# The opening of an attention stage: half-size weight loads, plain matmuls ahead of the first projection, and one score pair moved

## What is computed

```
xs = x * condT / sqrt(128)               (per sequence)
u  = (xs @ w0) / sqrt(sum((w0*s)^2)+eps) (demodulated)
q, k, v = u @ W_qkv                      (16 heads of 64)
p  = softmax(mask(q k^T / 8));  o = p @ v
x  = x + o @ W_out
f, i, h = gates of x;  scan over the 128 tokens
```

## Time and profile before

| | |
|---|---|
| median of 3 runs | 1012.3 us |
| the profiled execution: its own time | 1013.4 us |
| its span | 1012.1 us |
| PE busy | 969.6 us, 96% of the span |
| DVE busy | 869.5 us, 86% |
| ACT busy | 838.4 us, 83% |
| POOL busy | 488.1 us, 48% |
| granted TensorE clock, mean | 0.997 |

### The profile page before, as it was taken

How to read it: one execution, slowest core, us unless ns; L and a number is a source line. 1 busy time by engine, 2 the same in 40 slices (tenths; PEclk the granted TensorE clock), 3 DMA queues, 4 the chain that set the end, 5 groups by cost and what they waited for, 6 DMA issues and landing times.

```text
span 1012.1 us, 25907 instructions
## 1 busy us (share of the span) xinstructions
PE 969.6 (96%) x8939; PEld 789.5 (78%) x8939; DVE 869.5 (86%) x3687; ACT 838.4 (83%) x2232; POOL 488.1 (48%) x572
## 2 busy tenths in 40 slices
PE   7999999999999999899989999999999999999897
PEld 6899999998989899633268988888777777776566
DVE  6777989898989899599998999888989888896985
ACT  6999889898989889677797878776888888886786
POOL 2444656564646464416810112102888888893041
PEclk9999999999999999999999999999999999999999
DMA  9000000000000000000000000000000000000002
GB/s 381 31 2 2 2 2 2 2 2 1 3 2 2 2 2 2 1 1 1 1 1 1 1 1 1 1 11 12 22 23 23 23 23 22 24 3 2 1 1 84
DMA packets 8722, 18.30 MB, mean 18 GB/s; under 512 B 1296, under 2 KB 5648, under 8 KB 8208
## 3 DMA queue, kind: packets, MB, share of 16 engines
q1 hardware_dynamic: 8592, 16.65, 4.9%
HBM read 10.36 MB, written 2.10 MB: 12 GB/s over the span
## 4 chain that ended last, share of the span: by engine, by line
PE 69%; DVE 17%; ACT 6%; POOL 4%; issue 4%; DMA 0%; ACTq 0%; DVEq 0%; POOLq 0%
PE PB L258 7%; PE PB L259 6%; PE PB L260 6%; PE PB L1874 5%; PE PB L399 5%; PE PB L416 4%; PE PB L360 4%; PE PB L1259 3%; PE PB L1261 3%; PE PB L1260 3%; PE PB L1846 3%; PE PB L1891 3%; DVE AR_s L328 2%; DVE W L370 2%; PE PB L1904 1%
## 5 line engine op out<-in xcount | busy, mean ns | idle before, releaser
L258 PE MATMUL PB<-RR_s 128*128 128x256 f32 (+3 forms) x568 | 190.3, 335 | 4.8 <-POOL RR_s L479 1.9
L259 PE MATMUL PB<-RR_s 128*128 128x256 f32 (+3 forms) x568 | 176.8, 311 | 0.0
L260 PE MATMUL PB<-RR_s 128*128 128x256 f32 (+3 forms) x568 | 176.7, 311 | 0.0
L379 ACT ACTIVATE W<-W,small 128x128 f32<-128x128 f32 x384 | 149.0, 391 | 15.8 <-DVE small L370 15.8
L391 POOL TENSOR_TENSOR W<-W,small 128x512 f32<-128x512 f32 x96 | 100.1, 1046 | 105.9 <-DVE small L385 105.9
L1862 POOL TENSOR_TENSOR AR_s<-AR_s,small 128x512 f32<-128x512 f32 x128 | 129.4, 1041 | 15.1 <-DVE small L1855 14.9
L258 PEld LDWEIGHTS PB<-RR_s 128*128 128x128 f32 x568 | 108.4, 191 | 22.4 <-issue 8.8
L1233 ACT ACTIVATE AR_s<-PB,W 128x512 f32<-128x512 f32 (+2 forms) x160 | 100.5, 629 | 28.6 <-PE PB L260 22.7
L1247 DVE TENSOR_TENSOR RR_s<-AR_s,RR_s 128x512 fp32r<-128x512 f32 (+2 forms) x160 | 100.4, 637 | 17.0 <-ACT RR_s L1238 13.8
L1855 DVE CUSTOM_DVE_ANT_0 AR_s<-PB,W 128x128 f32<-128x128 f32 x512 | 111.2, 286 | 2.0 <-issue 0.2
L259 PEld LDWEIGHTS PB<-RR_s 128*128 128x128 f32 x568 | 108.6, 191 | 4.5 <-issue 0.5
(11 more groups left out here) (392 smaller groups left out, 2600.1 us busy)
## 6 DMA issues: line engine op xcount, KB each, us to landing
W<-in_w SPq DMA_DIRECT2D x1, 5809.5 KB, 24.5
W<-in_w SPq DMA_DIRECT2D x2, 1024.0 KB, 6.8
out<-XT SPq DMA_DIRECT2D x8, 256.0 KB, 2.3
XF<-in_xT SPq DMA_DIRECT2D x3, 512.0 KB, 9.9
W<-AR_s SPq DMA_DIRECT2D x16, 64.0 KB, 2.1
AR_s<-AR_s SPq DMA_DIRECT2D x16, 64.0 KB, 2.1
QS<-AR_s SPq DMA_DIRECT2D x12, 64.0 KB, 2.1
KR<-AR_s SPq DMA_DIRECT2D x12, 64.0 KB, 2.1
```

The lines of the kernel that those rows point to most:

```text
L258: nc.tensor.matmul(out, lh, rh, start=True, stop=False)
L259: nc.tensor.matmul(out, ll, rh, start=False, stop=False)
L260: return nc.tensor.matmul(out, lh, rl, start=False, stop=True)
L379: e = nc.scalar.activation(SS[r][:, hl], SS[r][:, hl], ACTF.Exp, bias=mx[r][:, h:h + 1], scale=-1.0, accum_out=rc[r][:, h:h + 1])
```

## The change

Five edits in the opening, and one that acts in the whole stage:

- wq and wk are stored as two halves (`wqk0`: the first 512 columns of each, `wqk1`: the last), loaded by two transfers of 512 KB with a semaphore each. The loads of x behind them are cut differently (1024 and 2048 columns instead of three times 1024).
- The factor -1/8 moves out of the weights' high and low parts into the maximum (`dve_max`), whose scale was 1.0; the mask's sign turns. `dve_weights` becomes a plain subtraction.
- Three of six low parts of weights go from DVE to POOL (`pool_weights`, entries 2 to 4), and the last one (entry 5) moves behind `dve_rc(1)` of period 0.
- The ten transposes become two groups of six plain 128x128 matmuls of ones, one ahead of the demodulation and one behind u.
- The fourth `pe_k` and its copy `dve_qk(3)` go behind the scores of units 0 and 1 and their maxima. ACT makes the first weights' high part ahead of `act_uh(0)`, and loads the exponential's table after the second.
- In every period `act_pt(4z-1)` now stands ahead of `act_xh`, where there is one.

```
-        nc.sync.dma_start(W1[:, 0:o_v], w_d[:, 0:o_v]).then_inc(s_w[0], 16)
+        nc.sync.dma_start(W1[:, 0:o_k], w_d[:, 0:o_k]).then_inc(s_w[0], 16)
+        nc.sync.dma_start(W1[:, o_k:o_v], w_d[:, o_k:o_v]).then_inc(s_w[4], 16)
...
+        def pool_weights(i):
+            name, at, landed, h, hi, lo = WEIGHTS[i]
+            pool.wait_ge(s_wh, i + 1)
+            nc.gpsimd.tensor_tensor(cs(lo, h), cs(w(name), at), cs(hi, h), ALU.subtract).then_inc(s_const, 1)
...
-                nc.vector.tensor_tensor_reduce(SS[r][:, hl], score(u, h), w("mask"), 1.0, 3.0e38, ALU.add, ALU.min,
+                nc.vector.tensor_tensor_reduce(SS[r][:, hl], score(u, h), w("mask"), -0.125, 3.0e38, ALU.add, ALU.min,
...
         def pe_attend():
+            pe.wait_ge(s_const, 4)
+            for k in range(6):
+                nc.tensor.matmul(PB[4][:, 0:128], ones, ones, start=True, stop=True)
             pe.wait_ge(s_set, 3)
             nc.tensor.matmul(PB[6][:, 0:32], w2, ys2, start=True, stop=True).then_inc(s_dem, 1)
             pe_u(0)
-            for k in range(10):
-                nc.tensor.transpose(PB[4][:, 0:128], ident, ident)
+            for k in range(6):
+                nc.tensor.matmul(PB[4][:, 0:128], ones, ones, start=True, stop=True)
             pe.wait_ge(s_dem, 2)
-            for n in range(4):
+            for n in range(3):
                 pe_k(n)
             for z in range(NP - 1):
                 for u in range(4 * z, 4 * z + 4):
+                    if u == 2:
+                        pe_k(3)
                     pe_S(u)
...
             nc.scalar.activation(dT, PB[6][:, 0:32], ACTF.Sqrt, bias=c_eps8).then_inc(s_dem, 1)
+            act_weights(0)
             act_uh(0)
-            for i in range(6):
+            act_weights(1)
+            nc.scalar.activation(pads[:, 2:3], pads[:, 3:4], ACTF.Exp)
+            for i in range(2, 6):
                 act_weights(i)
-            nc.scalar.activation(pads[:, 2:3], pads[:, 3:4], ACTF.Exp)
...
+                if z:
+                    act_pt(4 * z - 1)
                 for s in split_steps(2 * z + 1):
                     act_xh(*s)
-                if z:
-                    act_pt(4 * z - 1)
...
             dve_uf(0)
+            dve_weights(0)
             dve_ul(0)
-            dve_weights(0)
             dve_weights(1)
-            for n in range(4):
-                dve_weights(2 + n)
+            for n in range(3):
                 dve_qk(n)
             for z in range(NP):
                 dve_max(4 * z)
                 if z:
                     dve_rc(4 * z - 1)
                 dve_max(4 * z + 1)
+                if z == 0:
+                    dve_qk(3)
+                    dve_rc(0)
                 dve_max(4 * z + 2)
...
                 dve_rc(4 * z + 1)
+                if z == 0:
+                    dve_weights(5)
...
             pool_xs(0)
+            for i in range(2, 5):
+                pool_weights(i)
             pool_xs(1)
```

59 lines of the change are left out of this document (34 added, 25 removed).

## The result

| | before | after | ratio, 95% interval |
|---|---|---|---|
| median, us | 1012.97 (1011.80 to 1014.03, 7 runs) | 1017.34 (1014.54 to 1018.26, 7 runs) | 1.0032 (1.0020 to 1.0044) |
| the same kernel once more | 1013.53 (32 runs) | 1016.25 (1014.81 to 1018.16, 11 runs) | 1.0025 (1.0014 to 1.0036) |
| profiled execution, us | 1013.4, span 1012.1 | 1014.81, span 1013.5 | |
| mean granted clock | 0.997 | 0.997 | |

The forecast was 1013.5 with a range to 1015.6. The change makes the kernel **slower, by 2.7 to 4.4 us** at the medians; by the ratios it is 0.25 and 0.32%, about 2.5 and 3.2 us, with both intervals above 1. And yet the profiled execution came out where the sum had put it, at 1014.81 against 1014.6. That execution is among the shortest of its kernel.

The account below looks back on a forecast made before the run. From about 38 us PE's own work was taken as the bound, so the opening only makes everything start sooner. Reordering +2.89 less opening 1.67 is +1.22: 1014.6 us profiled, 1013.5 for the median, range 1010.1 to 1015.6.

Parts of the forecast that it names:

- rival 4: Opening: the half load brings nothing, first projection at 9.4, opening worth 0.4, 1014.8 us; chance 0.12.
- The clock, 2.4 GHz from 8.2 on: PE in the opening: matmuls of ones raise the clock early, 2.4 GHz from 8.2 us; other bound 9.6.
- The new wait: Opening: units 2 and 3 wait for DVE's fourth copy behind eight maxima; 1.9 of 3.55 us won given back.
- Scores of period 1, 20.91: PE, end of the opening: these scores start at 20.91 instead of 22.59 us, 1.68 earlier.
- Rival 3: Opening: ACT's earlier first exponential counts, gain 3.55 us, 1011.6 with the reordering; chance 0.08.
- Period 5, +0.53: Reordering in period 5: act_xh later, PE's gate projection at 82.12 instead of 81.59, +0.53 us.
- Periods 9 and on, 0.22 each: Reordering in periods 9, 13 to 29: act_xh 0.22 us later, all counting on PE, six times, +1.32.
- rival 1: The reordering is absorbed by PE's small waits in the next periods, 1010.6 us; chance 0.20.
- Period 31, +1.04: Reordering in the last period: POOL's low part of x, on the chain that ended last, 1.04 us later.
- The whole reordering, +2.89: act_pt ahead of act_xh over all periods: the period terms together cost 2.89 us.
- the opening is worth 1.67: All edits of the opening together: 1.67 us gained, 1.1 if the clock rises only at 9.6.
- Rival 2: Opening: matmuls of ones count no more than transposes, PE at 1.2 GHz until about 13.4, 1015.5 us; chance 0.13.

Follow-up runs that it names:

- xh_first: The changed kernel with the reordering undone, act_xh ahead of act_pt again, new opening kept: 1011.9 us (12 runs), ratio 0.9992.
- pt_first_only: The kernel before with only the reordering, act_pt ahead of act_xh, old opening kept: 1016.06 us (8 runs), ratio 1.0029.
- after_transposes: The changed kernel with the old warm-up, ten transposes in place of the matmuls of ones: 1016.12 us (12 runs), ratio 1.0016.
- look_b2: The kernel before, unedited, one more profiled execution: 1016.59 us.
- look_b3: The kernel before, unedited, another single profiled execution: 1012.63 us.
- look_a2: The changed kernel, unedited, one more profiled execution: 1016.2 us.
- xh_fill: xh_first with 14 instead of 6 matmuls of ones in the second warm-up group: 1012.55 us (12 runs), ratio 1.0001.
- look_a4: The changed kernel, unedited, another single profiled execution: 1016.17 us.
- after_fill: The changed kernel with 14 instead of 6 matmuls of ones ahead of the first projection (the filled kernel): 1017.48 us (11 runs), ratio 1.0026.

## Why the prediction was wrong, step by step

- **First projection, 8.19.** Right: 8.47 in the profile, 8.19 to 8.81 in the five executions, up to 9.23 in xh_first, as the load comes. The half load does what it should, and rival 4 is out.
- **The clock, 2.4 GHz from 8.2 on.** It was up by then in all fourteen executions with the matmuls of ones, between 4.2 and 7.3 us, though it did not stay up in all. No run shows the other bound, a rise at 9.6.
- **First scores 10.70, first maximum 11.92.** 10.92 and 12.13, the 0.2 to 0.3 of the first projection carried on.
- **The new wait.** Right: the copy ends at 14.52 (forecast 14.30), the next copies start at 17.47 (17.26).
- **Scores of period 1, 20.91.** 21.16 in the profile, so -1.43 of the forecast -1.67, of which 1.32 is the load. Rival 3, ACT's head start, is out: ACT waits 2.46 us for the first value projection, behind its eight exponentials, as was argued against it.
- **Period 5, +0.53.** From its scores to the next it takes 13.95 instead of 13.32 us, +0.63. **Periods 9 and on, 0.22 each.** 14.38 instead of 14.16 in period 9, and 0.2 in the others; but the period behind each is 0.1 shorter (13.05 instead of 13.14), so rival 1, the absorption, was right for about half of this term. Together +1.46 (+1.41 against xh_first) of the forecast 1.85.
- **Period 31, +1.04.** The low part is 0.98 later. Where no clock falls near 423 us the rest is 0.8 longer (608.3 in pt_first_only, 607.5 in xh_first).
- **The whole reordering, +2.89.** pt_first_only gives +2.9 with an interval from 1.4 to 4.4. By the parts it is 1.3 and 0.8, so 2.1 where no clock falls; what more there is comes with the fall near 423 us, which the sum did not have.

**The step that failed** is the term "the opening is worth 1.67", with "I take 2.4 GHz from 8.2 us on" under it, as a gain kept in every execution. Both ends of it were wrong. On the side of the changed kernel the clock does come up early, and then it falls again at about 15 us in three of five executions. The fall costs 0.95 us before the scores of period 1, which then stand at 22.12 to 22.45, and 0.5 more in period 1: 1.5 us gone of 1.67. On the side of the kernel before, the trace that I read had a late rise, at 13.5; in two of three executions it is up by 8.6, with the scores of period 1 at 22.43 and 21.98. Part of the forecast gain was in the kernel already.

By the middle values of the table the opening is worth 0.3 (22.43 to 22.12), not 1.67, the middle part costs 1.8 (381.09 to 382.86), and the rest 1.3 (608.5 to 609.8). That is +2.8, against +2.7 and +4.4 measured at the medians, and inside both ratios' intervals. With all executions that share an opening, four old ones and eight new ones, the opening is worth 0.8 (22.5 to 21.7), half of the term, less what a fall costs in period 1. What stays in every execution is the earlier load; the rest of the opening gained 0.1 us at most.

This accounts for the size of the miss and not for all of the spread. The filled kernel had no fall at 15 us in three executions and has the same median, and six runs of the changed kernel are longer than any that was profiled. How much of the medians the fall makes stays open.

The Trainium skill, page "TensorE: Matmul & The Clock Gate", Part 4, was cited for transposes that do not count as activity of PE. The one trace I had agreed with it as far as it went. The runs do not bear it out: with only ten transposes behind two products of 0.6 and 1.2 us the clock was up at 7.8 (after_transposes, during the last transpose), 8.6 (look_b2) and 8.4 (look_b3), and in three other executions of such an opening at 12.6, 13.5 and 13.9. The measurement decides: the clock can come up while PE transposes, and it did so early in three of six executions. How much the two products ahead of the transposes have to do with it no run separates. With the matmuls it was up between 4.2 and 7.3 us in all fourteen profiled executions that have them. Rival 2, matmuls of ones that count for nothing, is out.

A second, smaller fault: the term for period 31 was priced by the shift alone. The same shift of 1 us moves a wait of 2.7 us on PE, and along with it the clock falls near 423 us in ten of eleven executions, where it fell in four of nine; that the shift is the reason was not tested by itself. Without a fall up to 430 us the rest was 607.4 to 607.6 us with the high parts first and 608.3 with the transposed weights first, so without a fall the shift cost 0.8 of the forecast 1.04. With a fall near 423 us, none at 411 and none at 759 it was 608.5 and 609.0 in the one order, and 609.8 to 610.1 in the other.

A third is how the number was put on the median: 1.1 us below the profiled execution because before stood so. The changed kernel's median stands 2.5 above its profiled execution. One execution of each kernel says what the chain does, not how often the clock falls.

What stays open: the fall at 15 us follows the wait of 1.57 us, but a fill of that wait alone, of the right length, was not tried. Among the eight executions of the new opening, those with the fall had the rise at 4.5 to 5.0 us and those without it at 4.2 and at 5.8 to 7.3; so when the clock rose may matter, and eight are too few to tell. And the opening without the reordering is 1.6 and 1.0 us under the kernel before at the medians of two comparisons whose intervals both contain 1 (0.9992 and 0.9990): likely a gain, not a shown one. xh_first has the lowest median of this study, with 1011.9 against 1016.25 for the changed one beside it.

## What to carry to other kernels

A step that is put behind another one on its engine is paid for on the engines that wait for it, even if its own engine loses nothing: half a microsecond of ACT's order cost 2.1 us on PE and POOL by the traces, and 2.9 by the timed runs. Cut every trace at two or three fixed instructions and compare the parts of several executions before you trust a gain of 1 to 2 us; one trace of each kernel would have called this change +1.4. And a gain that creates idle time on PE in front of dense work has to carry the risk that the clock falls there: it did in four executions of fourteen with such a wait, though it was not shown that the wait is the cause.

## What the runs showed of the hardware

- The granted clock of one and the same program changes at other times in each execution: up at 13.5, 8.6 or 8.4 us in the kernel before; at 4.2 to 6.6 in the changed one, with or without a fall at 15. Without that fall the time from the scores of period 1 to the last scores hardly knows of it: 0.13 us of spread over nine executions.
- The load of the same 512 KB is not there at the same time either: the first high part starts at 5.79 to 6.42 us in the five executions of the changed kernel, and the scores of period 1 follow 15.1 us behind it, or 16.0 with the fall.
- Stretches at 1.2 GHz can be free. One or two of them near 950 us are in every execution, and executions that differ in their number there have the same rest (609.9 with one in the profile after, 609.8 with two in look_a2). So have those with a stretch at 505 to 510 us (607.4 in xh_fill, 609.8 in look_a4). A stretch at 759 goes with a rest that is 1.7 us and more longer (611.6 in after_fill).
- Three low parts of 128x512 on POOL took 3.77 us together, 1.26 each, where 1.28 were assumed. The timeline of POOL also shows the normalization, 1.04 us elsewhere, at 1.40 where DVE ran a subtraction of two SBUF operands beside it (L277, 0.66 from 18.76 on); one place, so a hint:

```profile
9.65 3.77 POOL L282 TENSOR_TENSOR RR_s<-W,RR_s 128x512 fp32r<-128x512 f32 x3 [5.31 <-ACT RR_s L272]
...
18.92 1.40 POOL L404 TENSOR_TENSOR W<-W,small 128x512 f32<-128x512 f32 x1 [3.20 <-DVE small L398]
20.69 1.04 POOL L404 TENSOR_TENSOR AR_s<-AR_s,small 128x512 f32<-128x512 f32 x1 [0.37 <-DVE small L398]
```
